# ScalarE writes odd relative-position tiles along their rows; the last batch's output steps are moved and its own output goes to VectorE

## The reference, cut to what matters

```
xn = layernorm(x)
scores = q k^T + rel_q + rel_k               # 16 heads of 16 numbers, 512 x 512 per head
ctx = softmax(scores / 4) v
s = layernorm(ctx Wo + bo + xn) * gamma + beta
g = silu(residual + top-2 mixture of 8 experts)
out = x + s * g
```

## Time and profile before

| | |
|---|---|
| median of 3 runs | 2009.68 us |
| the profiled execution | 2002.44 us |
| its span, first to last instruction | 2000.9 us |
| mean granted TensorE clock | 0.909 |
| busy: TensorE, VectorE, ScalarE, POOL | 1626.6, 1235.0, 1129.1, 560.9 us |
| position terms in `experts` | 460 to 1296 us |
| attention | 1304 us to the end |

### The profile page before, as it was taken

How to read it: one execution, slowest core, us unless ns; L and a number is a source line. 1 busy time by engine, 2 the same in 40 slices (tenths; PEclk the granted TensorE clock), 3 DMA queues, 4 the chain that set the end, 5 groups by cost and what they waited for, 6 DMA issues and landing times. The chain is left out here.

```text
span 2000.9 us, 32700 instructions
## 1 busy us (share of the span) xinstructions
PE 1626.6 (81%) x11256; PEld 1180.2 (59%) x11256; DVE 1235.0 (62%) x3009; ACT 1129.1 (56%) x1994; POOL 560.9 (28%) x662
## 2 busy tenths in 40 slices
PE   5758620787999899989999899759999999999981
PEld 3325320676788778877887788635555555555540
DVE  6755561621565546454646465758988888888860
ACT  2433310125656374736564556259888888888960
POOL 1352446320000000101000000014253654555454
PEclk9887655898999899999999999969999999999995
DMA  6463445996887897999887877689989989999931
GB/s 208 169 210 108 137 134 178 234 277 201 302 295 251 276 331 258 327 333 377 298 307 247 278 247 269 243 275 316 330 266 324 295 281 333 293 288 329 313 115 42
DMA packets 227381, 514.96 MB, mean 257 GB/s; under 512 B 37328, under 2 KB 83920, under 8 KB 222736
## 3 DMA queue, kind: packets, MB, share of 16 engines
q1 hardware_dynamic: 201856, 410.03, 63.6%
q0 software_dynamic: 24208, 98.65, 14.8%
q10 hardware_dynamic: 1152, 4.19, 0.5%
HBM read 367.08 MB, written 199.23 MB: 283 GB/s over the span
## 5 line engine op out<-in xcount | busy, mean ns | idle before, releaser
L983 DVE TENSOR_TENSOR rel_out<-rl,rel_tile 128x1024 f32<-128x1024 f32 x256 | 400.4, 1569 | 358.2 <-PE rl L1036 326.8
L960 ACT COPY rel_tile<-rl 128x1024 f32<-128x1024 f32 x256 | 377.0, 1476 | 297.7 <-DVE rel_out L983 164.7
L1273 ACT ACTIVATE scores<-scores,row_least 128x512 f32<-128x512 f32 x512 | 366.0, 718 | 35.5 <-DVE row_least L1309 33.2
L1309 DVE CUSTOM_DVE_ANT_1 scores<-sc,rq 128x512 f32<-128x512 f32 x512 | 338.6, 686 | 68.5 <-issue 57.7
L1413 PE MATMUL pt<-ident,scores 128*128 128x128 f32 x2048 | 321.9, 281 | 32.8 <-ACT probsT L1280 25.3
L1057 PE MATMUL up<-rowsT,w_b 128*128 128x256 f32 x1280 | 317.5, 394 | 4.4 <-DVE rowsT L989 2.3
L1413 PEld LDWEIGHTS pt<-ident,scores 128*128 128x128 f32 x2048 | 249.0, 145 | 115.7 <-DVE probsT L1317 35.9
L1070 PE MATMUL dn<-w_b,hid 128*128 128x256 f32 x1280 | 307.8, 385 | 0.0
L1057 PEld LDWEIGHTS up<-rowsT,w_b 128*128 128x128 f32 x1280 | 237.9, 195 | 33.8 <-DVE rowsT L989 5.0
L1070 PEld LDWEIGHTS dn<-w_b,hid 128*128 128x128 f32 x1280 | 233.1, 191 | 25.9
L1405 PE MATMUL sc<-ks,qs 96*128 96x512 bf16 x512 | 204.2, 399 | 32.9 <-DMA ks<-scratch_parts 20.0
(11 more groups left out here) (188 smaller groups left out, 1670.5 us busy)
## 6 DMA issues: line engine op xcount, KB each, us to landing
scratch_rel<-rel_out SPq DMA_DIRECT2D x256, 512.0 KB, 3.8
rq<-scratch_rel SPq DMA_DIRECT2D x256, 512.0 KB
krows_sb<-scratch_stack SPq DMA_DIRECT2D x768, 64.0 KB, 3.1
w_b<-in_w POOLq DMA_DIRECT2D x40, 1152.0 KB
w_b<-in_w POOLq DMA_DIRECT2D x40, 1028.0 KB
scratch_parts<-part SPq DMA_DIRECT2D x96, 128.0 KB
qrows_sb<-scratch_stack SPq DMA_DIRECT2D x192, 64.0 KB, 3.3
qs<-scratch_parts SPq DMA_DIRECT2D x192, 64.0 KB
```

Of the source, the lines that this page charges most:

```text
L960: nc.scalar.copy(square(tile)[:, :, u * UN:(u + 1) * UN], rl[r][:].rearrange("p a (b l) -> p l (a b)", l=TILE)).then_inc(s_kc, 1)
L983: nc.vector.tensor_tensor(out[n % SRING][:], rl[r][:].rearrange("p a (b s) -> p (a b) s", s=TILE), square(tile)[:, u * UN:(u + 1) * UN], A ...
L1273: nc.scalar.activation(sm[j][:, i], sm[j][:, i], ACT.Exp, bias=least[:, j, i:i + 1], scale=-1.0, accum_out=es[:, g // 2 % 2, i, 2 * j + g ...
L1309: nc.vector.tensor_tensor_reduce(sm[j][:, i].rearrange("p (c s) -> p c s", c=LT), sc[i % 2][:].rearrange("p (c s) -> p c s", c=LT), rq[j][ ...
```

## The change

There are four parts. First, in odd tiles ScalarE's copy goes through the unit in its own order: the same numbers go to the same places, and both the PSUM and the SBUF side are walked in adjacent numbers. Second, in the last batch (b = 7) the eight projection steps of batch 6 are at heads 4, 5, 5, 6, 7, 7, 8, 8, `add_rest` at 6 and 8, `statistics` at 7 and 9, `seed` at 10. Third, POOL no longer does `finish(7)`; after the reload it does `prepare(7)`, which makes `ax*gamma` in `ax` and `x + ax*beta` in `xx`. Fourth, VectorE does `finish_last`: subtract the mean and multiply by `ax*gamma`, the three Newton steps, and multiply by the root and add `xx`, each big step in four pieces of 128x256. SyncE stores the result in two halves.

```diff
-                        nc.scalar.copy(square(tile)[:, :, u * UN:(u + 1) * UN],
-                                       rl[r][:].rearrange("p a (b l) -> p l (a b)", l=TILE)).then_inc(s_kc, 1)
+                        if tile % 2 == 0:
+                            dst, src = both[:, :, u * UN:(u + 1) * UN], rl[r][:].rearrange("p a (b l) -> p l (a b)", l=TILE)
+                        else:
+                            dst, src = both[:, u * UN:(u + 1) * UN], rl[r][:].rearrange("p a (b l) -> p (a b) l", l=TILE)
+                        nc.scalar.copy(dst, src).then_inc(s_kc, 1)
...
-        PROJECTS = (4, 5, 6, 7, 9, 10, 11, 12)
+        PROJECTS, LAST_PROJECTS = (4, 5, 6, 7, 9, 10, 11, 12), (4, 5, 5, 6, 7, 7, 8, 8)
...
+            for half in range(2):
+                sp.wait_ge(s_fin, 2 * half + 2)
+                dst = t["out"][(B - 1) * S:B * S].rearrange("(p t) e -> p t e", t=ST)
+                sp.dma_start(dst[:, 2 * half:2 * half + 2], hh[:, 2 * half:2 * half + 2]).then_inc(s_end, 16)
+            sp.wait_ge(s_end, 32)
...
+            def prepare(b):
+                pool.wait_ge(s_g, b + 1)
+                pool.wait_ge(s_out, 16 * b)
+                step.did(nc.gpsimd.tensor_tensor(oo[:], ax[b % 2][:], over_tiles(gb[:, 1], ST), ALU.mult))
+                nc.gpsimd.tensor_tensor(ax[b % 2][:], ax[b % 2][:], over_tiles(gb[:, 0], ST), ALU.mult).then_inc(s_pre, 1)
+                step.settle()
+                pool.wait_ge(s_xx, (b + 1) * 16)
+                nc.gpsimd.tensor_tensor(xx[:], xx[:], oo[:], ALU.add).then_inc(s_pre, 1)
...
-            finish(B - 1)
-            pool.wait_ge(s_out, 16 * B)
+            prepare(B - 1)
+            pool.wait_ge(s_out, 16 * (B - 1))
...
+            def finish_last():
+                ve, a, y = (work[:, i] for i in range(3))
+                gain, rest = ax[(B - 1) % 2], xx
+                dve.wait_ge(s_pre, 2)
+                for i in range(ST):
+                    stat.did(nc.vector.scalar_tensor_tensor(hh[:, i], hh[:, i], mv[:, i, 0:1], gain[:, i], ALU.subtract, ALU.mult))
+                dve.wait_ge(s_seed, B)
+                for _ in range(3):
...
+                for i in range(ST):
+                    nc.vector.scalar_tensor_tensor(hh[:, i], hh[:, i], y[:, i:i + 1], rest[:, i], ALU.mult, ALU.add).then_inc(s_fin, 1)
...
+                adds, stats, seeds = ((7, 12), (9, 13), 14) if b + 1 < B else ((6, 8), (7, 9), 10)
+                if b and h in adds:
+                    add_rest(b - 1, adds.index(h))
+                if b and h in stats:
+                    statistics(b - 1, stats.index(h))
+                if b and h == seeds:
                     seed(b - 1)
...
             seed(B - 1)
+            finish_last()
...
+                for step in range(2 * ST):
+                    if b and h == (PROJECTS if b + 1 < B else LAST_PROJECTS)[step]:
+                        project(b - 1, step // 2, step % 2)
```

More of the change, by code:

```diff
@@ L1136, in attention @@
         s_seed, s_norm, s_pl = sem("root_seeded"), sem("out_normed"), sem("pool_steps")
+        s_pre, s_fin, s_end = sem("last_prepared"), sem("last_finished"), sem("last_stored")
         s_xo, s_xx, s_out = sem("xn_reloaded"), sem("x_reloaded"), sem("out_stored")
@@ L1364, in seed @@
                 nc.vector.tensor_scalar(y.bitcast(I32), a.bitcast(I32), -1, 0x5F3759DF, ALU.mult, ALU.add).then_inc(s_seed, 1)
+            def finish_last():
[6 more added lines that the diff above has]
+                for _ in range(3):
+                    stat.did(nc.vector.tensor_tensor(a, y, y, ALU.mult))
+                    stat.settle()
+                    stat.did(nc.vector.tensor_tensor(a, a, ve, ALU.mult))
+                    stat.settle()
+                    stat.did(nc.vector.tensor_scalar(a, a, -0.5, 1.5, ALU.mult, ALU.add))
+                    stat.settle()
+                    stat.did(nc.vector.tensor_tensor(y, y, a, ALU.mult))
+                    stat.settle()
+                for i in range(ST):
+                    nc.vector.scalar_tensor_tensor(hh[:, i], hh[:, i], y[:, i:i + 1], rest[:, i], ALU.mult, ALU.add).then_inc(s_fin, 1)
             for n in range(AHEAD):
@@ L1465, in _ @@
                     recip_rows(g // 2)
-                if b and h in PROJECTS:
-                    step = PROJECTS.index(h)
-                    project(b - 1, step // 2, step % 2)
+                for step in range(2 * ST):
+                    if b and h == (PROJECTS if b + 1 < B else LAST_PROJECTS)[step]:
+                        project(b - 1, step // 2, step % 2)
             for i in range(ST):
```

## The result

| | before | after |
|---|---|---|
| median | 2009.39 us (4 runs, 2003.91 to 2012.36) | 1954.83 us (4 runs, 1951.44 to 1960.8) |
| ratio | | 0.9724, 95% interval 0.9701 to 0.9748 |
| the profiled execution, its span | 2002.44, 2000.9 us | 1951.44, 1949.8 us |
| busy: TensorE, VectorE, ScalarE, POOL | 1626.6, 1235.0, 1129.1, 560.9 us | 1620.5, 1241.7, 1014.9, 545.5 us |

What follows compares the result with a forecast made beforehand. The prediction took TensorE as never resting in the position stretches and POOL's program order as deciding the end. Odd tiles -14 and the end -26 sum to -40 us: 1970 us forecast against a 2009.68 median, range 1957 to 1984.

Steps and rivals of the forecast that it cites:

- Odd tiles, forecast -14: Position terms: faster ScalarE copies bring eight plain odd stretches from 51.3 to 49.2 us, 17 less 3, so -14 us.
- rival (b): Odd stretches gain all of 22 to 27 us and the end's clock stays high, 3 us; 1957 us, chance 0.2.
- The upper end, 27: Odd stretches: bound on the gain if all TensorE idle time there went, 3.35 us times 8.
- The 3 us taken off for the queue: Odd stretches following query loads: ending sooner gives SyncE's late queue less time to get ahead; 3 us off the gain.
- the rule weighed there: Skill note: non-contiguous PSUM access is slow; for ScalarE's reads, the new copy would beat 1.01 us. Prediction: trace speaks against it.
- Moved steps, forecast -12.9: Last batch: batch 6's seed comes earlier, so POOL's wait before `finish(6)` goes; 12.9 us gained.
- rival (c): At the end, `finish(6)` beside busy VectorE is slowed by contention, giving back 9 of 26 us; 1979 us, chance 0.02.
- VectorE's finish, forecast -12.5: Last output: POOL's 18.0 us `finish(7)` leaves the path and 5.5 us on VectorE replace it.
- Low clock in the second half, forecast 6.4 us: Last projection's second half on TensorE runs at the low clock, 6.4 us; the other end is 3 us less.
- The halves, forecast -0.6: Last store: the first half goes out ahead, the second moves half the bytes; some 0.6 us less.
- The closing, forecast 0: After the last bytes: 8.9 us of receipt and closing that nothing here changes.
- The list of what would make the prediction wrong: Key-row waits growing as ScalarE's shrink, `last_prepared` ending VectorE's wait, or last result to end not about 11 us.

Runs made afterwards that it cites:

- experiment 9: Changed kernel with ScalarE's copies of even tiles reading PSUM in order and writing SBUF at a step of 128 numbers; 1963.71 us, ratio 0.9788.
- experiments 7: The changed kernel run again as it is; 1950.93 us, ratio 0.9711.
- 8: Changed kernel with one more wait at the end of POOL's program, for VectorE's last result; 1956.01 us, ratio 0.9712.
- experiment 12: Changed kernel with the last output stored in one piece in place of two halves; 1953.07 us, ratio 0.9702.
- experiment 11: Changed kernel with POOL issuing the reload of `xn` for the last output ahead of `finish(6)`; 1953.12 us, ratio 0.9715.
- experiment 5: Changed kernel with the two stores of the last output issued by POOL instead of SyncE's queue; 1950.48 us, ratio 0.9727.
- experiments 2: Changed kernel with the old ScalarE copy of odd tiles, so only the end is changed; 1967.59 us, ratio 0.9821.
- experiment 10: Changed kernel with VectorE's adds of odd tiles reading `rel_tile` in adjacent numbers, the step on output and PSUM; 1942.72 us, ratio 0.9674.
- 3: Kernel before with only the last batch's projection, adds, statistics and seed moved to their new places; 1990.23 us, ratio 0.9917.
- experiment 6: Kernel before with SyncE storing the last output in one piece after POOL's last addition; 2002.38 us, ratio 0.9972.

## Why the prediction was right in some of its parts and wrong in two, and in its sum

**Odd tiles, forecast -14: the step that failed is "what is on the path is the difference of the plain stretches, 51.3 - 49.2".** The duration of the new copy, 1.01 us, was exact. But a plain even stretch was the wrong floor for an odd one: in even stretches VectorE has its slow adds (34 us busy, here 1.92 us each), and TensorE rests for them. Once ScalarE's copies are fast, in an odd stretch neither helper is slow, and TensorE runs through in 46.4 us. That was rival (b)'s condition, with a chance of 0.2. Over all profiles, add to attention is 816.5 to 824.9 us with the old copy (5 kernels, mean 821.7) and 792.0 to 803.5 with the new one (8 kernels, mean 797.3): -24. The upper end, 27, held, but not for its reason: it counted TensorE's idle time as all there was to win, and 10.5 of the 23.3 us won were busy time. The 3 us taken off for the queue are not shown: even stretches sum to 368.2 to 374.5 us with the old copy and 371.5 to 376.3 with the new one, so the 3.3 of this profile are within the scatter.

The even copies settle the rule weighed there: in the order of PSUM reads nothing was to be had (experiment 9). What the odd copy paid for was its SBUF side. The Trainium skill ("Advanced Engine Details and Errata", Memory Cachelines) says that SBUF has lines of 16 bytes and that touching another line each time is penalised. The trace agrees: 1.92 against 1.01 us for ScalarE's writes, and 1.92 against 1.22 for VectorE's reads. The prediction had weighed only the PSUM half of the note that it cites.

**Moved steps, forecast -12.9: right.** POOL's wait of 12.96 us went (1909.17 without one), and the moved steps alone gave 14.4 us, 12.5 without the clock's 1.9. That the head loop is hardly disturbed was right too (0 to 1.5 us). So was rival (c)'s small chance: `finish(6)`, now beside a busy VectorE, took 18.1 us against 17.95.

**VectorE's finish, forecast -12.5: right.** From the seed's end, 1941.84, to the last result, 1947.37, it is 5.53 us against the forecast 5.5. Four of the big steps take 1.67 us, 0.42 each (taken: 0.37), the Newton chain 2.3 (2.4). `prepare` was done 2.9 us before VectorE asked (forecast 3, or just short with the high clock; it had the high clock and 2.9).

**Low clock in the second half, forecast 6.4 us: right in some executions, and which ones goes with the loop before.** At a pause of 0.78 to 0.79 us the second half stayed at 2.4 GHz in four profiles (the change, experiments 7, 8 and 12), fell midway in one (11) and was at 1.2 GHz throughout in one (5); at 1.41 to 1.65 it was low throughout in three (2, 9, 10) and fell midway in one (3). The pause itself goes with the last batch's head loop, though no experiment set the loop's clock. In the four with the long pause that loop ran at a granted clock of 1.00 and took 76 us; the reload then ends last, as the prediction drew it. In the six with the short pause the clock had fallen in the loop and it took 79.5 to 80.5 us; POOL is ahead, and the projection ends last (in experiment 11 the reload was early by design). So the 3 us that the profile of after has over the forecast came only behind a loop about 4 us longer. That where the clock falls varies, which the prediction took from the Trainium skill, is borne out by these ten; that an activity window runs freely, no run shows.

**The halves, forecast -0.6: right** (0.6, experiment 12).

**The closing, forecast 0: the second step that failed, "8.9 us of receipt and closing that nothing here changes".** The stretch was read rightly and put down to nobody. It is 7.9 us of DRAIN at the end of POOL's program, on the path only because POOL had the last work. Last result to end went from 11.6 to 2.4 us; less the 0.6 of the halves, 8.6 us that the sum did not have. The list of what would make the prediction wrong named this number ("isn't about 11 us"), though no rival stood behind it.

**The sum.** In the profiled executions -23 and -38, with +3.4 in a section that the change doesn't touch and +7.0 in one of which it touches the last batch alone. With the two failed steps put right, the forecast is -24 - 26 - 8.6 = -59, against a measured -54.6 (-51 to -60 by the interval of the ratio). The rest, some 4 us, was not traced; it is of the size of the scatter of the head loops, below. The errors were both on the side of too small a gain, 10 and 8.6 us, and so they added up beyond the range. Rival (b) came closest, 1957, with the right reason for its first half; its second, the high clock, stood in for the closing that it lacked, which is luck.

## What to carry to other kernels

The floor of a stretch from which one slow helper is taken is not a neighbouring stretch in which another helper is slow; look at what TensorE alone needs, and at the waits for loads for where it won't get there. Time behind the last transfer is somebody's: ask which engine's program ends last, look at the sequencer's records too, and have POOL end early. When ScalarE copies from PSUM to SBUF, walk SBUF in adjacent numbers and let PSUM take the step; for VectorE only the step on an SBUF source was priced by itself.

## What the runs showed of the hardware that was not expected

**POOL's closing.** From POOL's last operation or the end of its last wait to the end of the span: 8.0 us (experiment 6), about 8.3 from VectorE's last result for which POOL waits (8), 8.4 behind the last bytes before and 8.7 in experiment 5. Of these, 7.8 to 8.0 us are the DRAIN at the end of POOL's program. Where SyncE stores and POOL is done early, the end is 2.4 us behind VectorE's last result, transfer included. On ScalarE and VectorE the same instruction ends less than 0.1 us behind the last operation, and on SyncE it takes 0.1 us (before). Why POOL's is long was not looked into.

**The clock in the head loops.** TensorE pauses at each change of batch, and the granted clock may or may not fall. The last batch before, with 4 us near its start and the whole loop, and then after:

```profile
1860.50:1864.50 4.00, 2.98 (x23) 1.85 (x24) 3.27 (x14) 4.00 (x12) 2.04 (x11) 1.00 0.90 259
...
1856.50:1932.80 76.30, 71.21 (x486) 42.27 (x486) 68.18 (x244) 66.90 (x165) 41.38 (x48) 1.00 0.78 253
```

```profile
1843.30:1847.30 4.00, 3.01 (x13) 1.94 (x17) 2.92 (x12) 4.00 (x12) 2.07 (x11) 0.50 0.97 262
...
1839.30:1919.80 80.50, 75.17 (x486) 43.34 (x486) 68.80 (x247) 66.59 (x163) 50.73 (x65) 0.96 0.75 238
```

TensorE is busy 3 of the 4 us in both, yet in the second the clock is 0.50 and the loop 4.2 us longer. The moved steps alone don't make it: the same loop with them took 76.0 to 76.3 us at a clock of 1.00 (experiments 2, 3, 9 and 10). Over 98 such loops of 14 profiles, the 24 with a mean clock of 1.00 take 74.5 to 76.6 us (mean 75.2), the 41 with 0.98 a mean of 77.8, and the 33 with 0.96 a mean of 79.0. In each of the 74 the clock was low in one stretch alone, which began within 7 us of the loop's start. The clock can't be all of it: at 0.98 it takes 1.7 us of full speed from 78 us, and those 41 loops spread from 75.9 to 80.3 us. Seven loops an execution make up to some 27 us between all at 1.00 and all at 0.96 (7 x 3.8), which is enough for the spread of whole runs of one kernel (1934.5 to 1955.5 us in experiment 10), though no run shows that the spread is due to it. The last loop is 4.2 of the 7.0 us that the changed kernel's profile lost between attention's start and the last gate. Whether the fall can be prevented at the change of batch was not tried.
